# Two 64-wide self attentions of a transformer kernel: scores computed once and turned by TensorE instead of computed twice

## The reference

```
def mha(xq, ctx, wq, wk, wv, wo, bo):          # first block, self attention: ctx = xq
    q, k, v = heads(xq @ wq), heads(ctx @ wk), heads(ctx @ wv)      # 16 heads of 64
    scores = einsum('bhqd,bhkd->bhqk', q, k) / sqrt(64)
    out = einsum('bhqk,bhkd->bhqd', softmax(scores), v)
    return merge(out) @ wo + bo

# second block
q, k, v = heads(xn @ q_w + q_b), heads(xn @ k_w + k_b), heads(xn @ v_w + v_b)
q, k = rope(q, theta), rope(k, theta)
scores = where(causal, einsum('bhqd,bhkd->bhqk', q, k) / 8, -inf)
ctx = merge(einsum('bhqk,bhkd->bhqd', softmax(scores), v))
attn_out = ctx @ o_w + o_b + xn

x = x + L0_xcond(layernorm(x))   # self attention above, cross attention, GLU feed forward
x = x + L0_ffn(layernorm(x))     # causal attention above, then 31 small experts
x = x + L1_xcond(layernorm(x))   # six layers with 8-wide heads
x = x + L1_ffn(layernorm(x))     # 64 experts
```

## Time and profile before

| | us |
|---|---|
| median of 3 runs (lowest, highest) | 2603.01 (2599.17, 2604.14) |
| the profiled execution: span from first to last instruction | 2602.9 |
| PE busy | 2223.6 (85%) |
| DVE busy | 1696.5 (65%) |
| ACT busy | 1135.9 (44%) |
| POOL busy | 143.0 (5%) |
| mean granted clock of TensorE, as a share of full speed | 0.928 |

### The profile page before, as it was taken

One profiled execution on the slowest core, in us unless ns is written; L12 is line 12 of the kernel. 1 busy time (PEld: TensorE's weight loads), 2 busy tenths in 40 slices (PEclk: granted clock), 3 DMA queues, 4 the chain that ended last, 5 costly groups with the idle time before them and its releaser, 6 DMA issues.

```text
span 2602.9 us, 32241 instructions
## 1 busy us (share of the span) xinstructions
PE 2223.6 (85%) x11288; PEld 882.6 (34%) x11288; DVE 1696.5 (65%) x3941; ACT 1135.9 (44%) x1859; POOL 143.0 (5%) x143
## 2 busy tenths in 40 slices
PE   7999979889999898887887888788788878867898
PEld 3333333533333564223323222332322233232433
DVE  5767758646566687765774676577567557754464
ACT  3333323112223333563665466365546636654411
POOL 0000000011110201000000000000000000010000
PEclk9999989789999898888999799799979979988999
DMA  4000000200000100000000010010001000030000
GB/s 145 1 1 1 1 1 1 96 19 1 1 1 1 52 21 25 25 1 25 24 20 1 25 43 1 25 37 7 3 23 43 1 25 26 2 102 1 1 1 8
DMA packets 38032, 54.33 MB, mean 21 GB/s; under 512 B 5073, under 2 KB 34546, under 8 KB 36338
## 3 DMA queue, kind: packets, MB, share of 16 engines
q1 hardware_dynamic: 37874, 52.28, 6.4%
HBM read 32.34 MB, written 0.52 MB: 13 GB/s over the span
## 4 chain that ended last, share of the span: by engine, by line
PE 38%; DVE 10%; ACT 8%; issue 4%; SPq 1%; DMA 0%; ACTq 0%; DVEq 0%
PE ps L2084 7%; PE ps L2064 5%; ACT big L2569 4%; PE ps L2045 4%; DVE C_nm L2746 3%; PE ps L2212 2%; PE ps L2129 2%; PE ps L2319 2%; PE ps L2224 2%; ACT big L2649 2%; PE ps L2315 2%; PE ps L2340 2%; PE ps L2231 2%; PE ps L2240 2%; PE ps L2189 1%
## 5 line engine op out<-in xcount | busy, mean ns | idle before, releaser
L2746 DVE TENSOR_REDUCE C_nm<-ps 128x1 f32<-128x512 f32 x768 | 501.9, 685 | 185.6 <-PE ps L2045 180.9
L2569 ACT ACTIVATE big<-ps 128x512 f32<-128x512 f32 x768 | 427.7, 595 | 234.3 <-PE ps L2064 225.0
L2045 PE MATMUL ps<-C_attn 62*128 62x512 bf16 x768 | 276.5, 417 | 62.6 <-DVE C_nm L2746 51.6
L2064 PE MATMUL ps<-C_attn 64*128 64x512 bf16 x768 | 253.7, 398 | 62.1 <-ACT big L2569 51.8
L2084 PE MATMUL ps<-big,C_attn 128*32 128x512 f32 x1536 | 212.8, 627 | 13.3 <-ACT big L2569 13.3
L2045 PEld LDWEIGHTS ps<-C_attn 62*128 62x128 bf16 x768 | 63.2, 94 | 304.1 <-DVE C_nm L2746 165.7
L2064 PEld LDWEIGHTS ps<-C_attn 64*128 64x128 bf16 x768 | 59.3, 93 | 274.9 <-ACT big L2569 204.1
L2649 ACT ACTIVATE big<-ps,C_biasx 77x512 f32<-77x512 f32 x192 | 115.6, 679 | 56.4 <-PE ps L2216 56.3
L861 DVE TENSOR_REDUCE A_nm<-ps 128x2 f32<-128x1024 f32 x64 | 77.8, 1215 | 85.8 <-PE ps L609 85.5
L787 ACT ACTIVATE A_p<-ps 128x1024 f32<-128x1024 f32 x64 | 65.6, 1025 | 110.2 <-PE ps L637 110.2
L787 ACT ACTIVATE B_p<-ps 128x1024 f32<-128x1024 f32 (+1 forms) x64 | 45.0, 703 | 149.7 <-PE ps L641 149.7
(11 more groups left out here) (414 smaller groups left out, 3787.5 us busy)
## 6 DMA issues: line engine op xcount, KB each, us to landing
C_attn<-C_first SPq DMA_DIRECT2D x144, 128.0 KB, 2.4
C_w<-in_C_w SPq DMA_DIRECT2D x6, 1090.0 KB, 5.0
C_attn<-in_D_ew SPq DMA_DIRECT2D x4, 1536.0 KB, 10.9
big<-in_B_ew SPq DMA_DIRECT2D x8, 514.0 KB
normw_later<-in_norm_w SPq DMA_DIRECT2D x1, 2304.0 KB, 16.3
A_w<-in_A_w SPq DMA_DIRECT2D x2, 1024.0 KB, 11.6
A_w<-in_A_w SPq DMA_DIRECT2D x2, 768.0 KB, 8.6
B_w<-in_B_w SPq DMA_DIRECT2D x1, 1536.0 KB, 11.2
```

What stands on the lines that cost most here:

```text
L2045: pe.matmul(ps[:, bank, :], lhsT=qs[side(hp, MAX_ROW), b, 2 * q + pq, t * P:(t + 1) * P], rhs=ks[side(hp, MAX_ROW), b, 2 * q + pq, :], sta ...
L2064: pe.matmul(ps[:, bank, :], lhsT=ks[side(1 - hp, HALF), b, 2 * q + pq, kt * P:(kt + 1) * P], rhs=qs[side(1 - hp, HALF), b, 2 * q + pq, :], ...
L2569: act.activation(prob[:, kt % 2, pq, 1 - hp, :], ps[:, bank, :], ACT.Exp, scale=SCALE)\
L2746: dve.tensor_reduce(nm[:, q % 2, t, pq, hp:hp + 1], ps[:, bank, :], AX.X, ALU.max, negate=True).then_inc(emptied[bank], 1)
```

## The change

Scores are computed once, with the queries on the partitions. ScalarE takes the exponential of each head's 128x512 scores with the row's negative maximum as its per-partition bias and lets the same instruction sum the row (`accum_out`). The scale 1/8 moves into the copy of the queries (A1) or into tables of cosine and sine for the queries (B1: `cosq`, `sinq`). TensorE then turns the probabilities tile by tile (`turn`: 2 heads x 4 tiles a step in A1, 2 to 8 tiles in B1), VectorE copies the turned tiles from PSUM to SBUF (`copy_turned`), and the weighted sums come two steps later and a unit late, in two halves (`weigh(n, 0)` in step 2, `weigh(n, 1)` in step 3 of the next unit).

The inverse of the row sums is a 128x8 operation; GpSimd spreads it 64 wide (`widen`), TensorE turns it (`spread`), ScalarE copies it. The outputs of all eight pairs are kept (`cn`), and the output projection of a batch is done at once with the context as the stationary operand, so that it comes out with tokens on the partitions and is added to y without a transpose: for batch 0 in step 2 of unit 9, for batch 1 at the end. The tails, the angles and the sines move to other steps. The core of the diff, with the new order of each queue (the engine's name behind a line is added):

```diff
+            def turn(g):
+                n, t = divmod(g, TB)
+                pe.wait_ge(exp_done, 2 * (g + 1))
+                if g:
+                    pe.wait_ge(copied, g)
+                for h in range(2):
+                    for kt in range(tiles(t)):
+                        last = pe.transpose(ps[:, T_BANK + h, kt * P:(kt + 1) * P],
+                                            prob[:, g % 2, h, kt * P:(kt + 1) * P], m.ident[:])
+                last.then_inc(turned, 1)
...
+            def spread(n):
+                pe.wait_ge(widened, n + 1)
+                if n + 2 < N:
+                    keys_taken(n + 2)
...
+            def project_out(t, pairs, out):
+                for p in pairs:
+                    last = pe.matmul(out, lhsT=cn[:, p, t * P:(t + 1) * P], rhs=w[:, p, WO:WO + P],
+                                     start=p == 0, stop=p == PAIRS - 1)
...
+            for g in range(N * TB):                      # PE
+                u, t = divmod(g, TB)
...
+                if (u, t) == OUT_AT:                     # (9, 2)
...
+                if g >= 2:
+                    turn(g - 2)
+                scores(g)
+                if t == 0 and u + 1 < N:
+                    queries(u + 1)
+                if t == 1 and u + 1 < N:
+                    new_keys(u + 1)
+                if t == 2 and u:
+                    spread(u - 1)
+                    weigh(u - 1, 0)
+                if t == 3 and u:
+                    weigh(u - 1, 1)
+                if t == 3 and u + 1 < N:
+                    values(u + 1)
...
+            def exps(g):                                 # ACT
+                act.wait_ge(max_done, g + 1)
+                for h in range(2):
+                    act.activation(prob[:, g % 2, h, 0:keys(t)], ps[:, pair(g) + h, 0:keys(t)], ACT.Exp,
+                                   bias=nm[:, g % 2, h:h + 1], accum_out=sums[:, n % 2, t, h:h + 1])\
+                        .then_inc(exp_done, 1)
...
+            for g in range(N * TB):                      # DVE
+                u, t = divmod(g, TB)
...
+                if t == 0 and u >= 2:
+                    normalise(u - 2)
+                if g >= 2:
+                    copy_turned(g - 2)
+                row_max(g)
+                if t == 1 and u:
+                    invert(u - 1)
+                if causal and u + 1 < N and t < 2:
+                    rotate(u + 1, t, 0)
+                    rotate(u + 1, t, 1)
...
+            for n in range(N):                           # POOL
+                if causal:
+                    for i, (dst, ready) in enumerate(((qT, q_ready), (kT, k_ready))):
+                        pool.wait_ge(roped, n * 4 + 2 * i + 2)
+                        pool.tensor_tensor(dst[:, n % 2, :], rot[:, i, 0, :], rot[:, i, 1, :], ALU.add)\
+                            .then_inc(ready, 1)
+                if n >= 2:
+                    widen(n - 2)
...
-            def turn_max(n):
-            def scores_T(n, kt):
-            def denominators(n):
-            def split_max(n):
-            def add_up(n, kt):
```

More of the change, by code:

```diff
@@ L363, in later @@
                 norm.apply(dve)
+        for part in range(3):
+            if (u, kt) == (5 + part, 2):
+                self.angles(dve, part)
         if (u, kt) == (4, 2):
@@ L505, in self_attention_block @@
     SCALE = 0.125
-    S_BANK, ST_BANK, PV_BANK, OUT_BANK, MISC = 0, 2, 4, 6, 7
-    CONSTS = 4
-    keys = lambda t: (t + 1) * P if causal else S
+    S_BANK, T_BANK, PV_BANK, MISC = 0, 4, 6, 7
+    OUT_AT = (PAIRS + 1, 2)
+    tiles = lambda t: t + 1 if causal else TB
+    keys = lambda t: tiles(t) * P
     first_q = lambda kt: kt * P if causal else 0
     half = lambda h: slice(DH * h, DH * (h + 1))
+    pair = lambda g: S_BANK + 2 * (g % 2)
     ps = m.ps
[L513 to L522, removed]
-            nc.sbuf_tensor(name + "_den", [P, S], F32) as den, \
[L524 to L532, removed]
@@ L574, in k_first, with queries @@
[L574 to L592, removed]
+            def queries(n):
+                if n in (1, TB):
+                    pe.wait_ge(w_loaded[1 if n == 1 else 2], 16)
+                if n >= 2:
+                    pe.wait_ge(v_ready, n)
+                elif n == 1:
+                    pe.wait_ge(q_ready, 1)
+                project(n, WQ, q_done, bank_of(n, FIRST_Q, MISC))
+                if causal:
+                    if n >= 3:
+                        pe.wait_ge(cn_ready, n - 2)
+                    project(n, WQR, q_done, bank_of(n, FIRST_QR, PV_BANK))
@@ new lines, in weigh @@
+            def weigh(n, part):
+                if part == 0:
+                    pe.wait_ge(copied, (n + 1) * TB)
+                    pe.wait_ge(v_ready, n + 1)
+                    if causal:
+                        pe.wait_ge(roped, min(4 * (n + 2) + 4, 4 * N))
+                    if n:
+                        pe.wait_ge(cn_ready, n)
+                for kt in range(2 * part, 2 * part + 2):
+                    q0 = first_q(kt)
+                    for h in range(2):
+                        last = pe.matmul(ps[half(h), PV_BANK, q0:S], lhsT=v[:, n % 2, kt, half(h)],
+                                         rhs=pT[:, n % 2, h, kt, q0:S], start=kt == 0, stop=kt == TB - 1)
+                if part:
+                    last.then_inc(pv_done, 1)
@@ new lines, in _ @@
+                if (u, t) == OUT_AT:
+                    pe.wait_ge(cT_ready if causal else cn_ready, PAIRS)
+                    keys_taken(u + 1)
+                    for i in range(TB):
+                        last = project_out(i, range(PAIRS), ps[:, MISC, i * P:(i + 1) * P])
+                    last.then_inc(out_done, 1)
+                if g >= 2:
[5 more added lines that the diff above has]
+                    new_keys(u + 1)
@@ new lines, in _ @@
+            turn(N * TB - 2)
+            pe.wait_ge(ready, N - 1)
+            for t in range(2):
+                project_out(t, early, ps[:, t, 0:P])
+            turn(N * TB - 1)
+            for t in range(2, TB):
+                project_out(t, early, ps[:, t, 0:P])
+            spread(N - 1)
+            weigh(N - 1, 0)
+            weigh(N - 1, 1)
+            pe.wait_ge(ready, N)
+            for t in range(TB):
+                last = project_out(t, (PAIRS - 1,), ps[:, t, 0:P])
+            last.then_inc(out_done, 1)
```

637 lines of the change are left out of this document (251 added, 386 removed).

## The result

| | before | after |
|---|---|---|
| median of the runs, us (lowest, highest) | 2601.09 (2595.23, 2604.14), 4 runs | 2497.08 (2495.18, 2793.32), 4 runs |
| ratio | | 0.9595, 95% interval [0.9577, 0.9613] |

The change gains 4.1%, about 104 us. The forecast was 2521 with a range of 2490 to 2575. The highest of the four executions, 2793.32, had a granted clock of 0.16 in its last stage from about 2420 us on, which the change does not touch, and is left out of the ratio.

The account below looks back on a forecast made before the run. PE's queue was taken to bound both self attentions. From 2602.9 us, 33 came off for A1, 48 for B1 and 0.5 for stage C, giving 2521, with a range of 2490 to 2575.

Parts of the forecast that it names:

- Rival 3: Transposes and the wait in B1 drop PE's clock to 1.2 GHz, making the kernel slower, 2664 us; chance 0.06.
- Rival 4: Transposes in A1 and B1 do not overlap, each taking its whole 0.27 us: 119 more, 2640; chance 0.03.
- the signs: A1 unit 16.0 us, B1 16.85 with PE waiting 1.75 before `spread`, clock 1.00, cross attention at 302, stage C 81 earlier.
- A1, 278.5 predicted: A1 from first scores to the cross attention's first product falls from 311.7 to 278.5 us, a gain of 33.
- The kept part of the unit: In a unit of A1, the PE work that stays after the removed products: 10.98 us.
- The late projection: Batch 0's output projection, with nothing running under it: 8.5 us in A1, and 8.5 in B1.
- B1, 285.0 predicted: B1 with its end falls from 333.1 to 285.0 us, a gain of 48.
- The wait: In each B1 unit PE waits 1.75 us before `spread` for GpSimd's `widen`, queued behind the keys' rope addition.
- the sum of PE's work: PE work in a B1 unit: 11.74 us left, plus transposes 2.58, `spread` 0.5 and changes 0.3, making 15.1.
- The end of B1: The end of B1 takes 17.4 us; the old end was poor through late inversions, with PE mostly idle.
- Rival 1: The wait in B1 is hidden by VectorE's slack: 26 us less, 2495; chance 0.10.
- Rival 2: Eight transposes run slower, 0.20 us each, or the exponential chain becomes the bound: 58 us more, 2579; chance 0.17.

Follow-up runs that it names:

- turn_twice: The changed kernel with every transpose of probabilities done twice into the same place; 2580.59 us, ratio 0.9896.
- apart: widen_first with B1's four projection products placed on either side of the scores instead of in a row; 2477.91 us, ratio 0.9511.
- together: The changed kernel with both halves of a tile's weighted sums issued in one step; 2492.44 us, ratio 0.9565.
- again: The changed kernel run once more, unaltered, for a second profile; 2494.07 us, ratio 0.9562.
- the first execution: The changed kernel's first profiled execution, the highest of its four, with a low clock in the last stage; 2793.32 us.
- no_sums: The changed kernel without the sums that the exponential accumulates, a constant 1 in their place; 2488.71 us, ratio 0.9549.
- widen_first: The changed kernel with GpSimd's copy of the inverse sums moved ahead of the keys' addition in B1; 2471.2 us, ratio 0.9478.
- tail_moved: The changed kernel with VectorE's small router operations moved out of the steps where they stand behind the queries' rotation; 2488.86 us, measured once.
- both: widen_first with both halves of the weighted sums in one step; 2469.56 us, ratio 0.9482.

## Why the prediction was right, and where it was off

**What bounds.** Right. The queue of PE set both stages, and its full clock held but for a few us behind single waits, by `turn_twice` also with twice the transposes. Rivals 3 and 4 had the Trainium skill behind them (TensorE: Matmul & The Clock Gate, Part 4: PE-mode transpose). The trace agrees with its 275 ns as the duration of one transpose (0.273 for the float32 ones of L626), but they start 0.11 to 0.13 apart. That transposes do not count as activity is neither shown nor refuted: with 39% of A1's unit spent on them the clock is 1.00, but products stand between them. Of the signs, PE did wait for GpSimd in front of `spread`, and the first product of the cross attention came at 289.82 (302 forecast), stage C 109.7 earlier (81 forecast).

**A1, 278.5 predicted, 266.95 measured.** The kept part of the unit came out right (10.98 against 10.9: scores 4.24, projections 1.9, weighted sums 3.73, values 1.0), and that is luck in part: before, the scores took 3.84 and the others 7.14, so the scores, which now have products over 128 rows behind them and had `scores_T` over 64, got 0.40 dearer and the rest 0.48 cheaper. The transposes were not: 32 x 0.129 and 0.4 for the changes of product, 4.53, against 0.96 + 0.96 + 0.97 + 1.02 = 3.91 with the changes in it. `spread` was 0.59, not 0.5. So a unit is 15.4 for 16.0, 9 us over 15 units. The late projection took about 7.2 for 8.5 (64 products in 7.38 with the overlap), the end 15.7 for 17.1 (274.17 to 289.82). The first unit, 11 predicted, is about 10.8: the first `spread` starts at 40.71, and the scores of a unit start 7.04 before it (190.25 - 183.21).

**B1, 285.0 predicted, 264.3 measured.** The wait was forecast at its place and for its reason, at 1.75; it is 1.46 in eleven of the 15 units, 2.31 in two, and absent in two: unit 9, where the late projection comes first, and the last unit, as I had it. But the last unit is not the 7.0 shorter that I took off for it, only 5.2, for PE waits in it for ScalarE and VectorE. `widen` costs 0.61 (0.65 taken). The step that failed is the sum of PE's work, 15.1 against 13.7 to 13.9. The transposes with their changes are 2.62 for 2.58 + 0.3. The kept part is 10.53 where I had 11.74, and the missing 1.2 go with the order of the products: the four projections cost 3.55 (1.78 + 1.77) in pairs, and 4.08 one by one; the weighted sums 2.46 in two pieces and 2.74 in four; the masks 0.57 instead of 0.87, and three of the four are now followed by a product over 128 rows and not by `scores_T` over 64; the values 0.99 for 1.09. I added a price for each change of product that the new queue makes and took off none for those that the old one made. `apart` (0.30 a unit) and `together` (0.29 in B1, 0.15 in A1) show that order alone has such a price, some 0.6 of the 1.2; the rest, and its split, is read off distances and was not tested by itself. Outside the units, the late projection and the missing wait of unit 9 came out 2.6 under the 8.5, and the router's products, with the longer waits and the low clock behind one of them, some 2.5 over the 3.5.

**The end of B1.** Right in size (17.4 from the first of the last two `turn`s, 736.56, to 753.99), and one of its reasons was missing. The old end was poor not only for the inversions: PE, idle, worked there at the low clock. A stretch of the kernel before, and its timeline of PE:

```profile
848.00:856.00 8.00, 3.98 (x6) 0.79 (x6) 4.83 (x19) 1.32 (x2) 0.00 (x0) 0.52 0.00 0
```
```profile
859.03 2.07 PE L676 MATMUL ps<-B_cT,B_w 128*128 128x512 f32 x2 [5.63 <-ACT B_cT L800]
```

The same two products take 1.12 in the earlier trace rows. The old start was no better, which the prediction has nowhere: PE waited 1.77 and then 3.60 before the second unit's scores, and the clock was 0.50 from 542 to 550.

```profile
544.77 0.80 PE L609 MATMUL ps<-B_k,B_q 64*128 64x128 f32 x4 [3.60 <-issue]
```

The new start has neither. The forecast did not suffer by it, since its "now" is the whole measured stage and its "after" is added up afresh. The 28 early products of the new end ran at 1.00 in `again`; in the first execution the same products behind the same wait did not:

```profile
735.98 5.02 PE L677 MATMUL ps<-B_w,B_cn 128*128 128x128 f32 x28 [1.80 <-ACT B_cn L774]
```

**The rivals.** Rival 1 (wait hidden) did not come, though the total came near its 2495: two errors of the same sign, in A1 and in B1, stand in for it. So the result lies in the range (from 2490) by room that was kept for something that did not happen, and that is luck. Rivals 2 and 4 are out by the distances; the reading of the accumulator, 0.203 long where 0.2 was taken, costs ScalarE's queue less than half of that (two exponentials take 1.45 with it, 1.26 in `no_sums`). Rival 3 is out by the clock. The total of 2497 lies 24 under the forecast: A1 is 11.5 less and B1 18 (first execution) to 21 (`again`), nearly all of it PE's price of products, against which stands what single executions differ by elsewhere.

## What to carry to other kernels

When one queue is the bound, price a rewrite by distances from start to start, never by durations (a float32 transpose: 0.275 long, 0.12 apart), and take off the changes of product that go as well as adding those that come. Then look at the queue of the least busy engine: a copy of 0.61 us behind an addition that nobody needed yet cost 20 us in a stage that had gained 69, and one exchanged line gave it back.

## What was not expected of the hardware

VectorE and GpSimd stood in each other's way. An operation of 128x4 with two operands in SBUF took 1.26 us instead of 0.16 and ended with GpSimd's addition; moved away it took 0.16, and another one, beside GpSimd's copy, took 0.50. Copies from PSUM beside the same addition were not slowed (L831 of 128x1024 at 579.71 took 1.23, its mean is 1.225). The Trainium skill has the rule (SBUF — State Buffer, section "Who interferes with whom"): an instruction of VectorE with two inputs in SBUF contends with one of GpSimd that reads SBUF, over a pair of ports that is locked for one of them, and the order of issue decides which one blocks. These rows agree: L461 started 0.02 after GpSimd's addition and ended with it.

TensorE's granted clock fell behind short waits, and no length of wait tells when. In the five executions of this form of B1 (the first, `again`, `together`, `no_sums`, `tail_moved`) it fell behind one of 57 waits of 1.46 (in `tail_moved` at 653.27, where the eight products behind it took 3.02 for 1.65) and behind seven of eight of 2.31. Behind the 1.80 at the end of the stage it fell in the first execution and in `apart`, and not in `again`, `widen_first` and `tail_moved`. Behind a wait of 2.72 in `widen_first` it stayed, and that execution has 1.00 from the start to the end of B1. One such fall cost some 1.4 us (those eight products) to 2.9 (the 28 of `both`). So a wait taken out of PE's queue can be worth more than its length, and differs from execution to execution.
